# A ring of six rounded tiles in the second layer, with the steps of ScalarE and VectorE placed two tiles later

## What is computed

```python
ax1, ax2 = adj @ x, adj @ x2                     # first layer: both products
h1, h2 = 2 * ax1, 2 * ax2                        # (eps is 0)
for i in range(3):
    h1 = relu(h1 @ W1[i].T + b1[i]); h2 = relu(h2 @ W2[i].T + b2[i])
x = layernorm(x + concat(h1, h2) @ Wm.T + bm)
A = adj + eye(4096); d = A.sum(1) ** -0.5        # second layer
x = layernorm(x + (d[:, None] * A * d[None, :]) @ x @ W.T + b)
```

## Time and profile before

| | before |
|---|---|
| median of 3 runs | 609.15 us (608.16 to 609.58) |
| the profiled execution: its own time, its span | 609.65 us, 607.9 us |
| TensorE busy, share of the span | 589.8 us, 97% |
| VectorE | 546.0 us, 90% |
| ScalarE | 368.5 us, 61% |
| GpSimd | 27.6 us, 5% |
| chain that ended last, TensorE's share | 87% |
| DMA over the span | 141.56 MB, mean 233 GB/s |

### The profile page before, as it was taken

How to read it: one execution, slowest core, us unless ns; L and a number is a source line. 1 busy time by engine, 2 the same in 40 slices (tenths; PEclk the granted TensorE clock), 3 DMA queues, 4 the chain that set the end, 5 groups by cost and what they waited for, 6 DMA issues and landing times.

```text
span 607.9 us, 7948 instructions
## 1 busy us (share of the span) xinstructions
PE 589.8 (97%) x2660; PEld 481.2 (79%) x2660; DVE 546.0 (90%) x697; ACT 368.5 (61%) x446; POOL 27.6 (5%) x31
## 2 busy tenths in 40 slices
PE   4999999999999999999999999999989999999996
PEld 3888888888888888888888888867758778778885
DVE  5999988997988997998799999966898988998997
ACT  6454337753454773363676355585867787787783
POOL 1000000001100000110000110000200010010011
PEclk9999999999999999999999999999999999999998
DMA  8968555433554533455543376584779999899921
GB/s 294 414 238 284 201 209 202 144 139 139 202 187 176 197 138 138 140 205 207 182 163 138 150 282 242 210 332 167 272 292 344 342 386 392 341 309 392 385 103 37
DMA packets 27833, 141.56 MB, mean 233 GB/s; under 512 B 2592, under 2 KB 3360, under 8 KB 13600
## 3 DMA queue, kind: packets, MB, share of 16 engines
q1 hardware_dynamic: 27376, 139.67, 62.2%
q10 hardware_dynamic: 432, 1.57, 0.6%
HBM read 139.14 MB, written 2.10 MB: 232 GB/s over the span
## 4 chain that ended last, share of the span: by engine, by line
PE 87%; DVE 9%; issue 1%; DMA 1%; ACT 1%; POOLq 0%; POOL 0%; SPq 0%; DVEq 0%; ACTq 0%
PE ps L409 75%; DVE alo L733 6%; PE pd L427 6%; PE ps L485 3%; PE pd L438 2%; PE pd L471 1%; DMA raw<-a_t 1%; DVE stats L805 1%; DVE z L906 1%; ACT ahi L582 1%; DVE mv L813 0%; DVE x1lo L872 0%; DVE xn L874 0%; DVE raw L888 0%; DVE raw L895 0%
## 5 line engine op out<-in xcount | busy, mean ns | idle before, releaser
L582 ACT ACTIVATE ahi<-raw 128x1024 fp32r<-128x1024 f32 x253 | 265.5, 1059 | 209.6 <-PE ps L409 196.6
L733 DVE TENSOR_TENSOR alo<-raw,ahi 128x1024 fp32r<-128x1024 f32 x253 | 304.7, 1217 | 46.6 <-ACT ahi L582 45.6
L409 PE MATMUL ps<-ahi,x2s 128*128 128x512 f32 x512 | 160.0, 391 | 0.0
L409 PE MATMUL ps<-ahi,x1hi 128*128 128x512 f32 x448 | 145.3, 400 | 12.0 <-DVE alo L726 8.0
L409 PE MATMUL ps<-alo,x1hi 128*128 128x512 f32 x448 | 141.2, 391 | 0.0
L409 PE MATMUL ps<-ahi,x1lo 128*128 128x512 f32 x448 | 141.0, 391 | 0.0
L409 PEld LDWEIGHTS ps<-ahi,x2s 128*128 128x128 f32 x512 | 96.7, 189 | 20.2
L409 PEld LDWEIGHTS ps<-ahi,x1hi 128*128 128x128 f32 x448 | 82.4, 189 | 37.3 <-issue 13.3
L409 PEld LDWEIGHTS ps<-alo,x1hi 128*128 128x128 f32 x448 | 84.6, 189 | 17.8
L409 PEld LDWEIGHTS ps<-ahi,x1lo 128*128 128x128 f32 x448 | 84.4, 188 | 17.8
L409 PE MATMUL ps<-alo,x2s 128*128 128x512 f32 x256 | 80.7, 391 | 0.0
(11 more groups left out here) (80 smaller groups left out, 348.7 us busy)
## 6 DMA issues: line engine op xcount, KB each, us to landing
raw<-a_t SPq DMA_DIRECT2D x108, 1024.0 KB, 4.8
raw<-a_t SPq DMA_DIRECT2D x39, 512.0 KB, 7.4
xn<-x SPq DMA_DIRECT2D x3, 1024.0 KB, 8.2
out<-outn ACTq DMA_DIRECT2D x3, 512.0 KB, 4.1
par<-params SPq DMA_DIRECT2D x1, 708.0 KB, 13.8
xn<-x SPq DMA_DIRECT2D x2, 256.0 KB, 4.8
raw<-a_t SPq DMA_DIRECT2D x2, 256.0 KB, 5.0
xn<-x SPq DMA_DIRECT2D x1, 512.0 KB, 7.9
```

The source lines that it names most:

```text
L409: mm = pe.matmul(ps[bank][:, :], block_of(w, n), a[c], start=(n == 0 and k == 0), stop=(n == JB - 1 and k == 2))
L582: act.activation(ring_hi(n, last), raw_tile(layer, n), ACT.Copy).then_inc(hi_ready, 1)
L733: dve.tensor_tensor(ring_lo(n, last), raw_tile(layer, n), as_f32(ring_hi(n, last)), ALU.subtract).then_inc(lo_ready, 1)
```

## The change

- The second layer uses rings of six tiles (`SPLIT2`). Places four and five are the four 512-column parts of `hhi` and the two tiles of `alo_extra`; the row sums of the first layer's fourth quarter are turned into `outn` instead of `turned`, which lies under `alo_extra`. `used_ahead` gives the value of `block_used` that `round_a` waits for: tiles 0 to 3 of the second layer as before, tiles 4 and 5 nothing, later ones TensorE's tile n - 6.
- The steps of ScalarE and VectorE in the second layer stand two tiles later: `ACT_EVACUATE` 2 to 4, relus, residual, statistics, `ACT_NORM` 18 to 20, `ACT_COPY_AY` 1 to 3, `DVE_MAKE_Y` 22 to 24 (and with it `round_y` and `split_y`). TensorE's dense and merge steps stay, its projection moves from tile 1 to tile 2, and the output's residual on VectorE from step 5 to 8. In later quarters the identity is added five tiles early.
- TensorE's loop over the quarters 1 and 2 of the second layer is written out.

```diff
@@ -40,12 +40,12 @@
 RAW = 4
 RAW2 = 4
 SPLIT = 4
+SPLIT2 = SPLIT + 2
 LN_EPS = 1e-5
...
-EXTRA = JB - 2
...
 PE_DENSE = ({3: 0, 5: 1, 8: 2}, {1: 0, 3: 1, 5: 2})
 PE_MERGE = (10, 7)
-PE_PROJECT = 1
-
-
-ACT_EVACUATE = 2
-ACT_RELU = tuple({k + SPLIT: l for k, l in plan.items()} for plan in PE_DENSE)
-DVE_RESIDUAL = tuple(k + SPLIT for k in PE_MERGE)
+PE_PROJECT = 2
+
+
+AHEAD_OF_PE = (SPLIT, SPLIT2)
+ACT_EVACUATE = (2, 4)
+ACT_RELU = tuple({k + ahead: l for k, l in plan.items()} for plan, ahead in zip(PE_DENSE, AHEAD_OF_PE))
+DVE_RESIDUAL = tuple(k + ahead for k, ahead in zip(PE_MERGE, AHEAD_OF_PE))
 STATISTICS = (2, 4)
...
 DVE_TURN = (5, 4)
 DVE_BASE = (10, 7)
 DVE_SHIFT = tuple(k + 2 for k in DVE_AGGREGATE)
-ACT_NORM = (22, 18)
-ACT_COPY_AY = 1
-DVE_MAKE_Y = (KB + 4, 2 * KB + 4, 3 * KB + 4, 22)
+ACT_NORM = (22, 20)
+ACT_COPY_AY = 3
+DVE_MAKE_Y = (KB + 4, 2 * KB + 4, 3 * KB + 4, 24)
 ACT_ROUND_Y = tuple(k + 1 for k in DVE_MAKE_Y)
 DVE_SPLIT_Y = tuple(k + 2 for k in DVE_MAKE_Y)
 AHEAD = 3
-DVE_RESIDUAL2 = PE_PROJECT + SPLIT
+AHEAD2 = 5
+DVE_RESIDUAL2 = PE_PROJECT + SPLIT2
 DVE_STATISTICS2 = DVE_RESIDUAL2 + KB
 DVE_AGGREGATE2 = DVE_STATISTICS2 + KB // 2
 DVE_SHIFT2 = DVE_AGGREGATE2 + 3
...
-        alo_extra = sb("alo_extra", [P, JB - EXTRA, QW], F32R)
+        alo_extra = sb("alo_extra", [P, SPLIT2 - SPLIT, QW], F32R)
...
-        def ring_hi(n, last):
-
-            if last and n >= EXTRA:
-                m = 2 * (n - EXTRA)
+        def slot(layer, q, n):
+
+            return (q * JB + n) % SPLIT2 if layer == 1 else n % SPLIT
+
+        def ring_hi(layer, q, n):
+
+            i = slot(layer, q, n)
+            if i >= SPLIT:
+                m = 2 * (i - SPLIT)
                 return hhi[:, m:m + 2, :].rearrange("p m w -> p (m w)")
-            return ahi[:, n % SPLIT, :]
-
-        def ring_lo(n, last):
-
-            if last and n >= EXTRA:
-                return alo_extra[:, n - EXTRA, :]
-            return alo[:, n % SPLIT, :]
+            return ahi[:, i, :]
+
+        def ring_lo(layer, q, n):
+
+            i = slot(layer, q, n)
+            return alo_extra[:, i - SPLIT, :] if i >= SPLIT else alo[:, i, :]
+
+        def used_ahead(layer, q, n):
+
+            at = q * JB + (layer * QUARTERS * JB + n + 1)
+            if layer == 1 and q * JB + n >= SPLIT:
+                return at - SPLIT2 if q * JB + n >= SPLIT2 else 0
+            return at - SPLIT
...
-                hi = [ahi[:, n % SPLIT, c * CW:(c + 1) * CW] for c in range(CH)]
-                lo = [alo[:, n % SPLIT, c * CW:(c + 1) * CW] for c in range(CH)]
+                hi = [ring_hi(layer, q, n)[:, c * CW:(c + 1) * CW] for c in range(CH)]
+                lo = [ring_lo(layer, q, n)[:, c * CW:(c + 1) * CW] for c in range(CH)]
...
-                    if n == HALF_UNITS + PE_PROJECT + 2:
+                    if n == HALF_UNITS + PE_PROJECT + 1:
                         project(LAST, 1, range(KB // CH))
...
             layer1_quarter(0, None)
-            with pe.Fori(1, QUARTERS - 1) as q:
+            for q in range(1, QUARTERS - 1):
                 layer1_quarter(q, q - 1)
...
-                last = layer == 1 and q == LAST
-                if not (last and n >= EXTRA):
-                    wait(act, block_used, q * JB + (layer * QUARTERS * JB + n + 1 - SPLIT))
-                act.activation(ring_hi(n, last), raw_tile(layer, n), ACT.Copy).then_inc(hi_ready, 1)
+                wait(act, block_used, used_ahead(layer, q, n))
+                act.activation(ring_hi(layer, q, n), raw_tile(layer, n), ACT.Copy).then_inc(hi_ready, 1)
...
-                if n == ACT_EVACUATE:
+                if n == ACT_EVACUATE[plan]:
                     evacuate(q)
...
-                        if q == LAST and n == HALF_UNITS + SPLIT - 1:
+                        if q == LAST and n == HALF_UNITS + SPLIT2 - 1:
                             act.wait_ge(block_used, (QUARTERS + LAST) * JB + HALF_UNITS)
                             act.activation(h[:, 0, :], ps[0][:, :], ACT.Copy).then_inc(ay_copied, 1)
...
-                last = layer == 1 and q == LAST
                 wait(dve, hi_ready, q * JB + (layer * QUARTERS * JB + n + 1))
-                dve.tensor_tensor(ring_lo(n, last), raw_tile(layer, n),
-                                  as_f32(ring_hi(n, last)), ALU.subtract).then_inc(lo_ready, 1)
+                dve.tensor_tensor(ring_lo(layer, q, n), raw_tile(layer, n),
+                                  as_f32(ring_hi(layer, q, n)), ALU.subtract).then_inc(lo_ready, 1)
...
-                dve.transpose(turned[:, :], rowsum_all[:, :]).then_inc(turned_ready, 1)
+                dve.transpose((outn if q is LAST else turned)[:, :], rowsum_all[:, :]).then_inc(turned_ready, 1)
...
+                lines = (outn if q is LAST else turned)[:, :].rearrange("p (b r) -> p b r", r=TB)
+                dve.tensor_reduce(partial[:, :], lines,
...
                     if q == LAST:
-                        if n + AHEAD < JB and squares_of(n + AHEAD):
-                            add_identities_last(n + AHEAD)
-                    elif (n + AHEAD) // KB == q:
-                        add_identity(q, n + AHEAD)
+                        for i in range(0 if n == 0 else n + AHEAD2, min(n + AHEAD2 + 1, JB)):
+                            if squares_of(i):
+                                add_identities_last(i)
+                    elif q == 0:
+                        if n + AHEAD < KB:
+                            add_identity(q, n + AHEAD)
+                    elif (n + AHEAD2) // KB == q:
+                        add_identity(q, n + AHEAD2)
```

More of the change, by code:

```diff
@@ L478, in unit_products @@
                 c, j = unit(n)
-                hi, lo = ring_hi(n, True), ring_lo(n, True)
+                hi, lo = ring_hi(1, LAST, n), ring_lo(1, LAST, n)
                 for t in range(2):
@@ L617, in mlp_step @@
             def mlp_step(q, n, plan):
-                if n == ACT_EVACUATE:
+                if n == ACT_EVACUATE[plan]:
                     evacuate(q)
-                if plan == 0 and n in (ACT_EVACUATE + 1, ACT_EVACUATE + 2):
+                if plan == 0 and n in (ACT_EVACUATE[0] + 1, ACT_EVACUATE[0] + 2):
                     for m in range(CH):
-                        round_h(q, 0, CH * (n - ACT_EVACUATE - 1) + m)
+                        round_h(q, 0, CH * (n - ACT_EVACUATE[0] - 1) + m)
                 if n in ACT_RELU[plan]:
@@ L774, in turn_rowsums @@
                 wait(dve, raw_used, q * PAIRS + PAIRS)
-                dve.transpose(turned[:, :], rowsum_all[:, :]).then_inc(turned_ready, 1)
+                dve.transpose((outn if q is LAST else turned)[:, :], rowsum_all[:, :]).then_inc(turned_ready, 1)
             def add_turned(q):
                 wait(dve, turned_ready, q + 1)
-                dve.tensor_reduce(partial[:, :], turned[:, :].rearrange("p (b r) -> p b r", r=TB),
+                lines = (outn if q is LAST else turned)[:, :].rearrange("p (b r) -> p b r", r=TB)
+                dve.tensor_reduce(partial[:, :], lines,
                                   mybir.AxisListType.X, ALU.add).then_inc(partial_ready, 1)
@@ L829, in mlp_step @@
                 if plan == 0:
-                    if n in (ACT_EVACUATE + 1, ACT_EVACUATE + 2):
+                    if n in (ACT_EVACUATE[0] + 1, ACT_EVACUATE[0] + 2):
                         for m in range(CH):
-                            split_h(q, 0, CH * (n - ACT_EVACUATE - 1) + m)
+                            split_h(q, 0, CH * (n - ACT_EVACUATE[0] - 1) + m)
                     if n in ACT_RELU[0] and ACT_RELU[0][n] < LAYERS - 1:
```

## The result

| | before | with the change |
|---|---|---|
| median of 7 runs | 608.73 us (608.16 to 609.58) | 610.93 us (610.50 to 611.07) |
| ratio, 95% interval | | 1.0033 (1.0023 to 1.0043) |
| profiled execution: its own time, its span | 609.65 us, 607.9 us | 611.06 us, 609.3 us |

The time lies inside the range given, 0.9 us under its upper end; the likeliest case, 609.4 us and no change, was not what happened. It was the second rival, two falls of the clock.

What follows compares the result with a forecast made beforehand. TensorE, busy 97% of the span, was taken as the bound. Terms -3.7 - 1.0 + 2.9 = -1.8, plus 2.1 for one clock fall, gave +0.3 on 609.65; the median 0.5 lower: 609.4 us, range 606.9 to 611.8.

Steps and rivals of the forecast that it cites:

- the likeliest case: One fall of the clock, at tile 24 of the second layer's first quarter: 609.4 us, no change, chance 0.43.
- the second rival: Clock falls at the layer boundary as well as at tile 24, another 2.1 us: 611.5 us, chance 0.24.
- What the ring takes away: Second layer: TensorE's pauses in the later quarters go, -3.7 us, and the loss at tile 25, -1.0 us.
- The 4.3 us in front of tile 24 are gathered, not saved.: Second layer's first quarter: tile 24 waits for y, so TensorE's losses become one pause of about 4 us; gain 0.
- The boundary: Between the layers: bank copies behind the roundings of tiles 3 and 4 hold TensorE's tile 0, +2.9 us, 2.75 idle.
- Written-out loop, other buffers, loads: nothing.: Second layer: the change's other parts put at nothing, with 0.5 us allowed for instruction supply in the written-out quarters.
- The price of a fall: One clock fall behind a TensorE pause costs 2.1 us, three quarters of the start's 2.9; bounds 0 and 2.9.
- I expect the fall at tile 24 and not at the boundary.: Clock falls behind the 4.1 us pause at tile 24, +2.1 us, not behind 2.75 us idle at the layer boundary.

Runs made afterwards that it cites:

- evac2: The changed kernel with the layer boundary's bank copies back behind round_a of tile 2 instead of tile 4; 605.25 us, ratio 0.9938.
- best: The changed kernel with bank copies behind tile 2 and the chain to y drawn together, normalisations in two groups of four; 599.95 us, ratio 0.9855.
- before_evac3: The kernel before, ring of four, with the layer boundary's bank copies behind round_a of tile 3 instead of tile 2; 611.84 us, ratio 1.0048.
- before_unrolled: The kernel before with only TensorE's loop over quarters 1 and 2 of the second layer written out; 608.75 us, ratio 0.9993.
- fill: The changed kernel with twelve matmuls of unused result before tile 24 of the second layer's first quarter; 609.09 us, ratio 1.0001.
- ychain_only: Against `best`: the boundary's bank copies behind round_a of tile 4 instead of tile 2; 604.65 us, ratio 0.9929 to the kernel before.
- best_evac3: Against `best`: the boundary's bank copies behind round_a of tile 3 instead of tile 2; 602.97 us, ratio 0.9909 to the kernel before.

## Why the prediction was right in its parts and wrong in its likeliest case

- *What the ring takes away*, -4.7 us. Right: quarters of 39.45 us for 29 tiles without a pause, and 4.7 us less from tile 24 to the end once the fall is taken off. `evac2`, with only one fall against it, is 3.5 us faster than before (4.7 less a fall of 1.6 would be 3.1).
- *The 4.3 us in front of tile 24 are gathered, not saved.* Right: 26.1 us from the merge to tile 24, as before, and one pause of 4.04 us. `best` shows that the chain was what held it: with the chain shorter, the pause is gone.
- *The boundary*, +2.9 us. Right: 3.0, and the copies' place as its cause is shown by `evac2` and, with a ring of four, by `before_evac3`.
- *Written-out loop, other buffers, loads: nothing.* Right for the loop (`before_unrolled`); among the changed kernel's waits from 390 us on none is for a load of `raw`. The buffers were not tried apart, but the sum leaves nothing for them.
- *The price of a fall*, 2.1 us. Its basis was the start of the kernel and a fraction of it that was a guess. Measured were 1.6 and 2.5 in the profiled execution and 1.6 in `evac2`'s: none is 2.1, and that the first two average to it is luck.
- *"I expect the fall at tile 24 and not at the boundary."* This is the step that failed. The clock fell at both, which is rival 2: it gave +2.4 us against the median then known, and the medians differ by 2.2. I had one pause of 1.6 us that kept the clock and one idle stretch of some two microseconds that lost it, and wrote that 2.75 us of idleness lay between them. It lies above both. What was to set it apart was that a full stretch preceded it, and that no row showed: `before_evac3` shows a fall behind 1.87 us with a full stretch before it. The pause at the boundary should have been counted with those that fall. The range held only because it was drawn to take in this rival.

Only one of the changed kernel's seven runs was profiled. That both falls happen in all of them is likely: they lie within 0.6 us, and their mean granted clocks are 0.989 to 0.993, while no run of `evac2`, `fill` or `ychain_only`, each with one fall in its trace, is below 0.994.

## What to carry to other kernels

Here the deeper ring removed the pauses that came from a helper's bursts; it gathered those that came from a chain into one, and showed what the chain costs. When the steps of a table are moved by the depth of a ring, look at each for what it waited for: the copy that frees a bank hangs on TensorE's last tile, not on the ring, and has to stand in front of the first rounding that waits for that tile. In these kernels every profiled pause of 2.8 us or more cost 1.5 to 2.5 us on top, one of 1.87 us in one of two profiled executions, and those of 1.6 us or less nothing; where a pause cannot be removed, matmuls that nobody uses were cheaper.

## What the runs showed of the hardware

- A pause of 1.87 us idle in a full stream lost TensorE's clock in one execution (`before_evac3`, granted clock 0.50 from 398 to 400 us) and kept it in another (`best_evac3`, 1.00). Where it was lost, matmuls slowed down 1.2 us after TensorE had resumed (396.71 to 397.95).
- A fall cost between 1.5 us (`fill`, at the boundary: 396.93 to 401.26 for tiles 0 and 1) and 2.5 us here: matmuls of 512 columns about 0.43 us apart instead of 0.23, for one to two tiles.
- At the start of the kernel matmuls are 0.43 us apart for longer in one execution than in another: until the matmul at 14.08 in the earlier trace rows, and in the changed kernel's until about 12 us, which makes most of the 1.1 us of difference in a part that was not changed. That this is the low level of the clock is read from the spacing alone: the profile's own column of the granted clock stands at 1.00 from 8 to 14 us of the kernel before. The changed kernel's timeline of TensorE:

```profile
11.02 0.63 PE L422 MATMUL ps<-alo,x2s 128*128 128x512 f32 x1
...
12.14 0.39 PE L422 MATMUL ps<-alo,x2s 128*128 128x512 f32 x1
12.36 0.39 PE L422 MATMUL ps<-ahi,x2s 128*128 128x512 f32 x1
```

- The Trainium skill (TensorE: Matmul & The Clock Gate, "Why this matters for your kernels") warns of idle gaps between bursts of matmuls. These runs agree, and for shorter pauses than I had counted with: the clock fell behind 2.82 us in all three executions profiled with that pause (the changed kernel, `fill`, `ychain_only`), and behind 4.04 us in both (the changed kernel, `evac2`), where `fill` shows the same pause filled and no fall.
